# Windowed attention in a six-layer decoder block: value sums behind the scores, and the query norm as a row scale of the exponential

## The reference, cut to what matters

```
def attn_layer(x, Wqkv, qs, ksc, Wo):              # 16 heads of 64 channels
    q, k, v = split(x @ Wqkv)
    q = q / max(norm(q), 1e-12) * qs
    k = k / max(norm(k), 1e-12) * ksc
    q = q * cos * scale + rotate_half(q) * sin * scale
    k = k * cos * inv + rotate_half(k) * sin * inv
    sim = (q . k) * 8, masked: token i sees tokens i-32 .. i
    attn = softmax(sim); out = attn @ v
    return out @ Wo

for i in range(6):
    x = attn_layer(shift_tokens(x), ...) + x
    x = ffn_layer(shift_tokens(x), ...) + x
```

## Time and profile before

| | us |
|---|---|
| median of 3 runs | 4485.24 (4485.17 to 4485.28) |
| the profiled execution, its own time | 4488.07 |
| its span, first to last instruction | 4486.2 |
| stages A, B and what prepares the layers | up to 696 |
| one layer, windowed stage and MLP stage | about 631 |

### The profile page before, as it was taken

The page is one execution under the profiler, slowest core; times in us unless marked ns, Lnnn a source line. Parts: engine busy times, 40 slices in busy tenths (PEclk is TensorE's granted clock), DMA queues, the critical chain, the costliest instruction groups (busy, mean ns, idle before and its releaser), DMA issues.

```text
span 4486.2 us, 139641 instructions
## 1 busy us (share of the span) xinstructions
PE 4111.2 (92%) x49600; PEld 3199.2 (71%) x49600; DVE 3746.4 (84%) x8992; ACT 3570.6 (80%) x11591; POOL 3380.6 (75%) x2459
## 2 busy tenths in 40 slices
PE   7988877999979999889999889998899998899997
PEld 5666655777767777667777667776677776677776
DVE  7988878888768888778888678887788887788886
ACT  6888986889838989658888478987398886598993
POOL 4544457999749999669999489997599995699992
PEclk9999998999989999999999999999899999999998
DMA  3000000000000000000000000000000000000000
GB/s 79 0 0 1 0 7 9 0 0 0 1 25 2 0 0 0 6 20 1 0 0 0 6 21 0 0 0 6 20 1 0 0 0 6 6 1 0 0 1 20
DMA packets 31381, 26.75 MB, mean 6 GB/s; under 512 B 10308, under 2 KB 23490, under 8 KB 31170
## 3 DMA queue, kind: packets, MB, share of 16 engines
q1 hardware_dynamic: 31170, 24.02, 1.9%
HBM read 21.92 MB, written 2.10 MB: 5 GB/s over the span
## 4 chain that ended last, share of the span: by engine, by line
PE 36%; issue 26%; POOL 17%; DVE 16%; ACT 3%; POOLq 1%; SPq 0%; DVEq 0%; DMA 0%; ACTq 0%
PE bank L668 7%; POOL rotated L1076 6%; POOL rotated L1096 6%; PE bank L760 5%; PE bank L661 5%; PE bank L738 4%; PE bank L724 4%; POOL rnorm L1084 4%; PE pair L826 3%; DVE by_cos L1328 3%; DVE top L1286 3%; DVE by_sin L1336 2%; PE bank L840 2%; DVE qk_parts L1261 2%; DVE qk_t L1434 1%
## 5 line engine op out<-in xcount | busy, mean ns | idle before, releaser
L1084 POOL TENSOR_TENSOR rnorm<-norm2g,neg_half 128x16 f32<-128x16 f32 x384 | 1116.3, 2907 | 227.4 <-DVE norm2g L1353 227.3
L1076 POOL TENSOR_TENSOR rotated<-by_cos,by_sin 128x512 f32<-128x512 f32 x768 | 983.3, 1280 | 180.1 <-DVE by_sin L1336 172.8
L969 ACT ACTIVATE pair<-pair,top 128x128 f32<-128x128 f32 x3072 | 1059.3, 347 | 0.7 <-DVE top L1360 0.6
L1096 POOL TENSOR_TENSOR rotated<-rotated,rnorm 128x512 f32<-128x512 f32 x768 | 787.0, 1047 | 0.5
L1328 DVE TENSOR_TENSOR by_cos<-bank,rot_cos 128x512 f32<-128x512 f32 x768 | 531.2, 692 | 259.5 <-PE bank L668 249.1
L986 ACT ACTIVATE prob_t<-bank 128x512 f32<-128x512 f32 x768 | 459.7, 599 | 258.7 <-PE bank L724 258.0
L969 ACT ACTIVATION_READ_ACCUMULATOR pair<-pair,top 128x1 f32 x3072 | 656.1, 214 | 0.0
L668 PE MATMUL bank<-wqkv_high,xt_high 128*128 128x512 f32 (+1 forms) x1536 | 593.8, 387 | 34.3 <-ACT squares L960 33.0
L1378 DVE TENSOR_TENSOR prob<-pair,rsum 128x512 f32<-128x512 f32 x768 | 531.1, 692 | 41.3
L661 PE MATMUL bank<-cst,rotated 128*128 128x128 f32 x3072 | 505.5, 287 | 48.1 <-POOL rotated L1096 43.5
L760 PE MATMUL bank<-wo_sb,vout 128*128 128x128 f32 x3072 | 548.1, 301 | 0.0
(11 more groups left out here) (154 smaller groups left out, 8453.3 us busy)
## 6 DMA issues: line engine op xcount, KB each, us to landing
wqkv_sb<-in_L_ffn_Wqkv_dram SPq DMA_DIRECT2D x36, 256.0 KB, 4.1
wo_sb<-in_L_ffn_Wo_dram SPq DMA_DIRECT2D x48, 64.0 KB, 2.0
out_dram<-y SPq DMA_DIRECT2D x8, 256.0 KB, 3.5
w_sb<-in_L_ffn_W_dram SPq DMA_DIRECT2D x6, 341.0 KB, 3.1
w_sb<-in_L_ffn_W_dram SPq DMA_DIRECT2D x12, 64.0 KB
cst<-in_constants_dram SPq DMA_DIRECT2D x1, 582.0 KB, 3.5
b_sb<-in_L_ffn_b_dram SPq DMA_DIRECT2D x1, 384.0 KB
w_sb<-in_L_ffn_W_dram SPq DMA_DIRECT2D x6, 42.5 KB
```

Of the source, the lines that this page charges most:

```text
L969: last = nc.scalar.activation(at, at, ACT.Exp, bias=top[jl % 2][:, h:h + 1], accum_out=psum_raw[jl % 2][:, h:h + 1])
L1076: nc.gpsimd.tensor_tensor(rotated[j % 4][:, :, :, :], by_cos[j % 2][:, :, :, :], by_sin[j % 2][:, :, :, :], ALU.add).then_inc(c_rot, 1)
L1084: nc.gpsimd.tensor_tensor(rnorm[slot][:, :, :].rearrange("t g n -> t (g n)"), norm2g[slot][:, :, :].rearrange("t g n -> t (g n)"), neg_hal ...
L1096: nc.gpsimd.tensor_tensor(at, at, rnorm[slot][:, i, :].unsqueeze(2).to_broadcast([P, 2 * HG, DH]), ALU.mult).then_inc(c_unit, 1)
```

## The change

Three things, all in the windowed stage.

1. The inverse norm of the queries no longer goes into the queries. `win_unit` on POOL multiplies the 256 key columns of a group alone. The scores then lack that factor. DVE's row maximum goes to a new tile `top_raw`, a new small operation `win_top` multiplies it by the inverse norm of the queries (a positive number, so the maximum stays the maximum), and the exponential takes the inverse norm as a per-row `scale`, read from `rnorm`. The ring `rnorm` grows from 2 to 4 tiles, and POOL waits for the exponentials that read a tile before it writes it again.
2. The probabilities are transposed one step later (`WIN.probs` 6 becomes 7), directly behind `win_project`, and copied by ACT directly behind the exponentials.
3. `win_sum_values` stands directly behind `win_scores` on PE, ahead of `win_heads`. On ACT the copy of the values stands ahead of the copy of the heads. On DVE the maximum stands behind `win_sin`.

```
-    probs = 6
+    probs = 7
-        rnorm = ring("rnorm", 2, [P, 2, 2 * HG])
+        rnorm = ring("rnorm", 4, [P, 2, 2 * HG])
+        top_raw = ring("top_raw", 2, [P, HG])
@@ PE, win_heads and win_turn_probs
-                    if has(it * STEPS + j - 1 - WIN.probs):
-                        pe.wait_ge(c_pt, g + WIN.turn - WIN.probs)
-                    elif has(it * STEPS + j - WIN.turn - 1):
+                    if has(it * STEPS + j - WIN.turn - 1) and not here(it, j, WIN.probs):
                         pe.wait_ge(c_qk, g)
-                    if here(it, j, WIN.turn):
-                        pe.wait_ge(c_qk, layer * GROUPS + it * STEPS + j - WIN.turn + 1)
+                    if here(it, j - 1, WIN.turn):
+                        pe.wait_ge(c_qk, layer * GROUPS + it * STEPS + j - WIN.turn)
@@ PE, win_step
                 win_project(layer, it, j)
+                win_turn_probs(layer, it, j)
                 win_values(layer, it, j)
                 win_mask(layer, it, j)
                 win_scores(layer, it, j)
+                win_sum_values(layer, it, j)
                 win_heads(layer, it, j)
-                win_sum_values(layer, it, j)
                 win_project_out(layer, it, j)
                 win_turn_next(layer, it, j)
-                win_turn_probs(layer, it, j)
@@ ACT, win_exponentials
-                        last = nc.scalar.activation(at, at, ACT.Exp, bias=top[jl % 2][:, h:h + 1], accum_out=psum_raw[jl % 2][:, h:h + 1])
+                        q = h % 2 * 2 + h // 2
+                        last = nc.scalar.activation(at, at, ACT.Exp, bias=top[jl % 2][:, h:h + 1], scale=rnorm[jl // 2][:, jl % 2, q:q + 1],
+                                                    accum_out=psum_raw[jl % 2][:, h:h + 1])
@@ ACT, win_step
                 win_exponentials(layer, it, j)
+                win_copy_probs(layer, it, j)
                 win_square(layer, it, j)
+                win_copy_values(layer, it, j)
                 win_copy_heads(layer, it, j)
-                win_copy_values(layer, it, j)
                 win_copy_next(layer, it, j)
-                win_copy_probs(layer, it, j)
@@ POOL, win_rnorm and win_unit
+                    if has(it * (STEPS // 2) + j // 2 - 4):
+                        pool.wait_ge(c_exp, 2 * u - 6)
-                        at = rotated[(j - 2) % 4 + i][:, :, :, :].rearrange("t a h d -> t (a h) d")
-                        nc.gpsimd.tensor_tensor(at, at, rnorm[slot][:, i, :].unsqueeze(2).to_broadcast([P, 2 * HG, DH]), ALU.mult).then_inc(c_unit, 1)
+                        at = rotated[(j - 2) % 4 + i][:, 1, :, :]
+                        nc.gpsimd.tensor_tensor(at, at, rnorm[(j // 2 - 1) % 4][:, i, HG:].unsqueeze(2).to_broadcast([P, HG, DH]), ALU.mult).then_inc(c_unit, 1)
@@ DVE, win_max (now into top_raw, with c_top_raw) and the new win_top
+            def win_top(layer, it, j):
+                if here(it, j, WIN.top):
+                    ...
+                    dve.wait_ge(c_top_raw, m + 1)
+                    nc.vector.tensor_tensor(top[jl % 2][:, :].rearrange("q (e i) -> q e i", e=2), top_raw[jl % 2][:, :].rearrange("q (e i) -> q e i", e=2),
+                                            rnorm[jl // 2][:, jl % 2, 0:HG].rearrange("q (i e) -> q e i", e=2), ALU.mult).then_inc(c_top, 1)
@@ DVE, win_step
                 win_cos(layer, it, j)
                 win_sin(layer, it, j)
+                win_max(layer, it, j)
                 win_recip(layer, it, j)
+                win_top(layer, it, j)
                 win_scale(layer, it, j)
                 win_norms(layer, it, j)
-                win_max(layer, it, j)
                 win_clamp(layer, it, j)
```

More of the change, by code:

```diff
@@ L368, in build @@
         c_scores = sem("c_scores")
+        c_top_raw = sem("c_top_raw")
         c_top = sem("c_top")
@@ L1083, in win_rnorm @@
                     slot = j // 2 % 2
-                    nc.gpsimd.tensor_tensor(rnorm[slot][:, :, :].rearrange("t g n -> t (g n)"), norm2g[slot][:, :, :].rearrange("t g n -> t (g n)"),
+                    if has(it * (STEPS // 2) + j // 2 - 4):
+                        pool.wait_ge(c_exp, 2 * u - 6)
+                    nc.gpsimd.tensor_tensor(rnorm[j // 2 % 4][:, :, :].rearrange("t g n -> t (g n)"), norm2g[slot][:, :, :].rearrange("t g n -> t (g n)"),
                                             neg_half[:, :], ALU.pow).then_inc(c_rn, 1)
@@ L1090, in win_unit @@
                     u = layer * UNITS + it * (STEPS // 2) + j // 2 - 1
-                    slot = (j // 2 - 1) % 2
                     pool.wait_ge(c_rn, u + 1)
@@ L1359, in win_max @@
                     dve.wait_ge(c_scores, m + 1)
-                    nc.vector.tensor_reduce(top[slot][:, :].rearrange("q (e i) -> q e i", e=2), win_ps[slot].rearrange("q e (i k) -> q e i k", i=2),
-                                            AX_X, ALU.max, negate=True).then_inc(c_top, 1)
+                    nc.vector.tensor_reduce(top_raw[slot][:, :].rearrange("q (e i) -> q e i", e=2), win_ps[slot].rearrange("q e (i k) -> q e i k", i=2),
+                                            AX_X, ALU.max, negate=True).then_inc(c_top_raw, 1)
+            def win_top(layer, it, j):
+                if here(it, j, WIN.top):
+                    m = layer * GROUPS + it * STEPS + j - WIN.top
+                    jl = (j - WIN.top) % STEPS
+                    dve.wait_ge(c_top_raw, m + 1)
+                    nc.vector.tensor_tensor(top[jl % 2][:, :].rearrange("q (e i) -> q e i", e=2), top_raw[jl % 2][:, :].rearrange("q (e i) -> q e i", e=2),
+                                            rnorm[jl // 2][:, jl % 2, 0:HG].rearrange("q (i e) -> q e i", e=2), ALU.mult).then_inc(c_top, 1)
             def win_recip(layer, it, j):
```

## The result

The changed kernel takes 4670.15 us (median of 4 runs, 4669.13 to 4672.18), the kernel before 4485.26 us on the same chip: 1.041 times as long (95% interval 1.0399 to 1.0425), 185 us more. The forecast was 301 us more, 4786, with a range of 4690 to 4880: the direction is right and the new loop is there, but the forecast is 116 us too high and the time lies outside the range.

The account below looks back on a forecast made before the run. PE's gapless list and a loop through ACT and PE were taken to bound the step. The new loop's 4.33 plus 0.15 gives 4.48 us against 4.075; 0.405 x 124 x 6 = 301 us more, 4786 us, range 4690 to 4880.

Parts of the forecast that it names:

- The new loop through L738: ACT and PE: exponentials, prob_t copy, L738, L661, heads' copy, next exponentials; 4.33 us a plain step.
- the round trip alone, at a free scale: ACT and PE: the loop with unscaled exponentials, 3.96 us, is already longer than the old step; 28 us more.
- The price of the row scale: ACT: a second per-row operand costs each exponential 0.09 us, four 0.37 us, none hidden between neighbours.
- The free case: Rival, 5%: on ACT the scale costs the exponentials nothing; loop 3.96 us, 28 us more, 4513 us.
- the half price: Rival, 7%: second operand partly read beside the accumulator's read, 0.045 us each; 167 us more, 4652 us.
- the term for the block of exponentials: ACT: four exponentials, start to the next instruction, grow from 1.53 to 1.90 us.
- the old loop "through ACT and PE": Exponentials, square, heads' copy, bank3, L724, prob_t copy, next exponentials; holds a plain step at 3.85 us.
- the fourth step: Each fourth step, token transposes on PE and a copy on ACT add 0.61 us, 0.15 a step on the mean.
- PE's wait for POOL: PE's 43.5 us wait for win_unit counted as gone, with halved columns and PE asking later.
- DVE covered: DVE: win_top's 0.1 to 0.3 us and at most 0.1 more for win_clamp fit in the step; cost zero.
- The clock did not fall: Rival, 4%, was that PE's waits lower its clock half the time; some 450 us on top, about 5200 us.
- The faster rival: Rival, 3%: PE's shorter list sets the pace, ACT never waits for L738 and L661; 134 us less, 4351 us.

Follow-up runs that it names:

- e4: Changed kernel with the value sums and output projection one step later, so L738 reads a prob_t copied in the step before; 4507.94 us.
- e7: e4 with one edit, top_raw in PSUM, so win_top reads one operand from SBUF and one from PSUM; 4320.07 us.
- e9: Changed kernel with top_raw in PSUM and nothing else; 4669.00 us.
- e2: Kernel before with the new PE, ACT and DVE order alone: no per-row scale, no win_top, POOL normalises queries and keys; 4393.15 us.
- e8: e1 with top_raw in PSUM, the inverse norm of the queries still left out; 4391.71 us.
- e3: Kernel before, with the exponentials taking a per-row scale that is a column of ones; 4618.57 us in the repetition.
- e1: Changed kernel without the exponentials' per-row scale, win_top multiplying by ones, inverse query norm left out of the computation; 4505.3 us.
- e5: Kernel before with the edits of e2 and e4 together: new order alone, value sums one step later; 4289.31 us.

## Why the prediction failed, step by step

**The new loop through L738: right, and shown.** The trace has each of its links; e4 takes L738 out of it and gains 162 us, e7 against e9 349 us. PE's wait at L738 was forecast at about 0.5 us a step, which is 384 us in 768 steps, and is 377; ACT waits 0.34 us before the values' copy (0.3 forecast). Against the forecast, the page shows no wait worth the name before the heads' copy (4.0 us in all): the values' copy starts 0.13 us after L738's end, where a hand-over to ACT was taken as 0.04, and so fills it. The claim that the round trip alone, at a free scale, is longer than the old step and costs 28 us was wrong: e2 and e8 are 92 and 94 us faster than before.

**The price of the row scale: right.** 0.09 us an exponential forecast, 433 - 347 = 86 ns measured, 1.74 - 1.37 = 0.37 us a step. The free case and the half price fall (e8 against e9, and 433 ns in e3). Here the rule that speaks of a free affine (the Trainium skill, ScalarE: Activation LUTs, *Step-by-step: what each stage is for*) does not hold as a price: e8 and e9, which differ in the scale (and in the second operand of `win_top`, which takes 0.16 us in both), are 277 us apart.

**The step that failed: the term for the block of exponentials, "from 1.53 to 1.90".** I took 1.53 us, start to start, for work. It held 0.16 us of waiting for `by_sin`, hidden under the accumulator's read. The work was 1.37, and with the scale 1.74, as e2 and the changed kernel show. For the same reason the old loop "through ACT and PE" of the prediction closes at 3.85 us only with that wait inside it, and ACT's room in a step was 0.52 us and not 0.36. 0.16 x 744 steps are 119 us, and 301 - 119 = 182, against the measured 185. The smaller errors nearly cancel, which is luck: the hand-over to PE was 0.05 and not 0.08, the last copy 0.50 and not 0.48, the fourth step added 0.66 us on the mean and not 0.61 (eight steps of the trace take 34.61 us, 4.327 each, and 4 x 4.16 + 0.66 = 17.30 are half of that). The bounds did not have this case: they varied the price of the scale and the hand-overs, and took the base of the term as read. Two slips in the working, 0.61 us where 1.78 - 1.18 gives 0.60 and 4700 beside 4690 for the foot of the range, weigh nothing here.

**PE's wait for POOL counts as gone: right,** 43.5 us became 4.3. What POOL's halved multiply is worth in the changed kernel was not tried; e8 has it and is no faster than e2, which has not.

**DVE covered: right for the changed kernel, by more luck than reason.** `win_top` was put at 0.1 to 0.3 us. It takes 0.16, or 0.57 to 0.65, and in e1 and e4 up to about 1.06 and 1.08 in the steady steps. e9 shows that the changed kernel does not feel it. In e1 and e4, where the loop is shorter, it costs 114 and 188 us (e8, e7).

**The clock did not fall:** the mean granted clock is 0.97 over the span as before, 0.98 in the first layer's windowed stage with PE busy 89% of it, and 1.00 from 1500 to 1660 us.

**The faster rival** described another kernel: one in which ACT never waits for L738 and L661, at 3.90 us a step and 4351 us with the scale, 3.88 by PE's list alone. With the loop cut and `win_top` short, e7 takes 3.88 us a step and 4320.07 us with the scale, e5 3.84 without it.

## What to carry to other kernels

A pipeline whose stages are all nearly always busy is priced by its loops, not by its busy times: follow each wait that the new order makes until it comes back to the same engine, and give a hand-over a step of lag where the loop exceeds the step. The price of an operation depends on whether it lies in that loop: the same scale cost 277 us inside it, and 31 us, with all of part 1, once the loop was cut. Before a start-to-start distance is used as the price of a block, look whether the next instruction was released by someone else at just that moment; two rows of the same instruction in another place tell it. And look at a small added operation for what its engine shares with a neighbour, not for its size alone.

## What the runs showed of the hardware

DVE's multiply of 128x4 with both operands in SBUF took 0.16 us beside POOL's `rnorm` (a power of 128x16, 2.91 us), all 372 times in the changed kernel. When it began during POOL's addition of 128x512 (1.28 us) it ended 0.02 us after that addition, all 361 times. With one operand in PSUM it took 0.16 us always (e7). The Trainium skill (GPSIMD Engine Reference, *Specifications*) names contention of GpSimd with VectorE operations of two SBUF inputs, which the long rows bear out; by the same skill (SBUF — State Buffer, *Terms*) the pair of ports is held for a whole instruction and the loser blocks fully. For the addition that is what the rows show, for the power of 2.91 us it is not.

A second per-row operand costs an exponential with accumulation 0.09 us (347 to 433 ns); the same step lies between a Gelu with one and an Identity with two, without accumulation.
